# Second attention: maxima read from two PSUM banks and one in turn, and the values' products cut into two halves of 256 columns

## The reference

```python
query = qt_c + qt_r                   # each heads(...): (b, 16, 1024, 8)
key = kt_c + kt_r
attn = jnp.einsum('bhqd,bhkd->bhqk', query, key) / scale      # scale = 12
attn = jax.nn.softmax(attn, axis=-1)
out = jnp.einsum('bhqk,bhkd->bhqd', attn, value)
```

## Time and profile before

| what | us |
|---|---|
| median of three executions | 2005.73 |
| lowest, highest | 2004.09, 2005.89 |
| profiled execution, span from first to last instruction | 2004.5 |
| second attention, its maxima's first to last product | 1129.7 to 1808 |
| steps, from the first exponential to the last reduce of a maxima tile | 1172.8 to 1809 |

### The profile page before, as it was taken

One profiled execution on the slowest core, in us unless ns is written; L12 is line 12 of the kernel. 1 busy time (PEld: TensorE's weight loads), 2 busy tenths in 40 slices (PEclk: granted clock), 3 DMA queues, 4 the chain that ended last, 5 costly groups with the idle time before them and its releaser, 6 DMA issues. The chain is left out here.

```text
span 2004.5 us, 34034 instructions
## 1 busy us (share of the span) xinstructions
PE 1788.9 (89%) x12761; PEld 670.6 (33%) x12761; DVE 1459.2 (73%) x3121; ACT 1092.4 (54%) x1386; POOL 644.9 (32%) x776
## 2 busy tenths in 40 slices
PE   6878799999999999999599888888888888889897
PEld 3535333333333333333333332111211211112465
DVE  5866666666666667663444689999999999994743
ACT  4312244454455445545324158878887878887432
POOL 0033445445555555432224113203302500001153
PEclk8987999999999999999799899999999999999798
DMA  4000000000000000000121101211221212220114
GB/s 137 1 1 1 1 21 25 23 24 23 23 24 23 34 24 24 33 24 23 24 111 54 62 26 69 74 44 44 81 81 45 86 65 63 82 81 7 63 35 145
DMA packets 56673, 91.80 MB, mean 46 GB/s; under 512 B 21989, under 2 KB 30565, under 8 KB 56381
## 3 DMA queue, kind: packets, MB, share of 16 engines
q1 hardware_dynamic: 54940, 85.94, 12.4%
q0 software_dynamic: 1280, 2.62, 0.5%
q10 hardware_dynamic: 288, 1.05, 0.2%
HBM read 46.23 MB, written 38.51 MB: 42 GB/s over the span
## 5 line engine op out<-in xcount | busy, mean ns | idle before, releaser
L1853 DVE TENSOR_REDUCE h_m_half<-h_ps_max 128x1 f32<-128x512 f32 x1024 | 635.8, 682 | 32.4 <-PE h_ps_max L1460 29.7
L1709 ACT ACTIVATE h_P<-h_ps_st 128x1024 f32<-128x1024 f32 x512 | 497.8, 1023 | 86.6 <-PE h_ps_st L1476 84.0
L929 PE MATMUL l_ps_st<-l_Q,l_K 64*128 64x512 f32 (+3 forms) x1536 | 310.3, 498 | 4.2 <-DMA l_Q<-l_m_row 2.0
L1089 ACT ACTIVATE l_P<-l_ps_st 128x1024 f32<-128x1024 f32 (+3 forms) x256 | 207.7, 834 | 192.7 <-PE l_ps_st L929 192.0
L1180 DVE CUSTOM_DVE_ANT_0 l_masked<-l_ps_t,l_mask 128x384 bf16<-128x384 f32 (+3 forms) x512 | 229.3, 485 | 63.7 <-PE l_ps_t L883 63.6
L1486 PE MATMUL h_ps_o<-h_P,h_V 128*9 128x512 f32 x2048 | 267.7, 595 | 0.7 <-ACT h_P L1709 0.5
L1460 PE MATMUL h_ps_max<-h_K,h_Q 48*128 48x512 bf16 x1024 | 201.0, 389 | 66.7 <-DVE h_m_half L1853 64.7
L1183 DVE TENSOR_REDUCE l_m_half<-l_ps_t 128x1 f32<-128x512 f32 x256 | 164.5, 685 | 69.7 <-PE l_ps_t L883 68.3
L1476 PE MATMUL h_ps_st<-h_Q,h_K 51*128 51x512 bf16 x1024 | 167.4, 379 | 14.9 <-ACT h_P L1709 11.0
L1460 PEld LDWEIGHTS h_ps_max<-h_K,h_Q 48*128 48x128 bf16 x1024 | 49.2, 93 | 387.1 <-DVE h_m_half L1853 372.5
L1757 POOL CAST h_m_parts<-h_m_neg 128x16 bf16<-128x16 f32 x32 | 6.3, 198 | 517.3 <-DVE h_m_neg L1817 517.3
(11 more groups left out here) (469 smaller groups left out, 2416.2 us busy)
## 6 DMA issues: line engine op xcount, KB each, us to landing
sums<-l_o SPq DMA_DIRECT2D x15, 512.0 KB, 2.7
sums<-h_o SPq DMA_DIRECT2D x15, 512.0 KB, 2.6
h_K<-k_parts SPq DMA_DIRECT2D x32, 192.0 KB
h_Q<-q_parts SPq DMA_DIRECT2D x32, 192.0 KB
y_rows<-zero SPq DMA_DIRECT2D x8, 512.0 KB, 4.9
c_W<-c_W SPq DMA_DIRECT2D x32, 128.0 KB, 2.1
c_W<-in_W SPq DMA_DIRECT2D x16, 256.0 KB, 4.0
c_back<-y_rows SPq DMA_DIRECT2D x16, 256.0 KB, 5.6
```

The costliest lines, as they stand in the source:

```text
L929: last = pe.matmul(ps_st[x % 2][:, a, 0:w], K[n // NG % 2][rows, kt * 128:(kt + 1) * 128], Q[n % NQ][rows, c, p, q0 - c * CH:q0 - c * CH + ...
L1089: act.activation(P[e % PR][:, :, 0:w], ps_st[slot["s", n, i, p] % 2][:, :, 0:w], ACT.Exp, scale=0.125).then_inc(consumed, 1)
L1709: act.activation(P[e % PR][:, :, :], ps_st[x % 2][:, :, :], ACT.Exp, scale=1.0 / 12.0).then_inc(consumed, 1)
L1853: dve.tensor_reduce(m_half[:, half, 2 * p + a, qt:qt + 1], ps_max[:, t % NB, :], AX.X, ALU.max, negate=True)\
```

## The change

Tiles are grouped in units: a unit of two tiles (banks 0 and 1), then a unit of one (bank 2), in turn; 683 units for 1024 tiles. DVE reads a unit with one `tensor_reduce`, 1024 or 512 wide. PE may write unit k when unit k - 2 is reduced, and signals once a unit. The results go to `m_tiles`, laid out by tile; `settle` combines them with two instructions of half the size where one was.

`values(n, i, side)` does the four products of a step for 256 of the 512 columns; the two sides are called apart. `next_maxima` has four places in a step: 0 between the scores, 1 after them, 2 between the sides, 3 after the second side. BEAT says which are used: 0, 2, 3 in two steps of three, and 1, 2 in the third; eight units, twelve tiles, in three steps. Every step has place 2. AHEAD = 53 bounds how far maxima run ahead: a place is left empty when the next tile's number isn't below 53 + 4 times the step's number. A step with a projection or an output has place 3 in any case, and there and after its product the bound doesn't hold. SKIP is gone.

The lead has the same 48 tiles in 32 units: 21 units (12 with half a `normalise`, 9 with two idle products), then the 12 idle products and the first turn, then 11 units with two idle products each (8 pairs before).

```diff
-    LEAD, TURNS, INVERT_AT = 8, (6, 14), 8
+    TILES, UNITS = 2 * NPAIR, 2 * (2 * NPAIR * NGR // 3) + 1
+    LEAD, TURNS, INVERT_AT = 32, (6, 14), 8
+    BEAT, AHEAD = ((0, 2, 3), (0, 2, 3), (1, 2)), 53
-    NORM_AT = {2 * k: x for k, x in enumerate(NORM)}
+    NORM_AT = {k + k // 3: (NORM[k // 2], k % 2) for k in range(2 * len(NORM))}
+    NORM_AFTER = {k + 2: x for k, (x, half) in NORM_AT.items() if half}
+    def tiles_of(k):
+        t = 3 * (k // 2) + 2 * (k % 2)
+        return range(t, t + 1) if k % 2 or k == UNITS - 1 else range(t, t + 2)
...
+            def maxima(k):
+                if k >= 2:
+                    pe.wait_ge(reduced, k - 1)
+                for t in tiles_of(k):
...
+                    last = pe.matmul(ps_max[:, t % NB, :], Q[n % NBUF][rows, p, qt * 128:(qt + 1) * 128],
+                                     K[n % NBUF][rows, p, lo:lo + CH], start=True, stop=True)
+                last.then_inc(max_ready, 1)
...
+            def values(n, i, side):
...
                 for j in range(HG):
-                    last = pe.matmul(ps_o[32 * j:32 * j + M, :], V[b % 2][:, kt, g * HG + j, :],
-                                     P[(2 * (n * NI + i) + j // 2) % PR][:, j % 2, :], start=(kt == 0), stop=(kt == KT - 1))
-                last.then_inc(pv_done, 1)
+                    last = pe.matmul(ps_o[32 * j:32 * j + M, cols], V[b % 2][:, kt, g * HG + j, :],
+                                     P[(2 * (n * NI + i) + j // 2) % PR][:, j % 2, cols], start=(kt == 0 and side == 0), stop=(kt == KT - 1 and side == 1))
+                if side:
+                    last.then_inc(pv_done, 1)
...
                     scores(n, i, 0)
-                    if follows:
-                        next_maxima()
+                    if 0 in beat:
+                        next_maxima(most)
                     scores(n, i, 1)
-                    if not follows and (n, i) not in SKIP:
-                        next_maxima()
+                    if 1 in beat:
+                        next_maxima(most)
                     if n + i:
-                        values(n if i else n - 1, (i - 1) % NI)
-                    next_maxima()
+                        values(n if i else n - 1, (i - 1) % NI, 0)
+                    if 2 in beat:
+                        next_maxima(most)
+                    if n + i:
+                        values(n if i else n - 1, (i - 1) % NI, 1)
+                    if 3 in beat or key:
+                        next_maxima(most if key is None else 2 * NPAIR * NGR)
...
+                tiles = m_tiles[:, at:at + TILES // 2].rearrange("x (k p s a) -> x p a k s", k=KT // 2, p=2, s=2)
+                for p in range(2):
+                    last = dve.tensor_tensor(m_neg[c][:, 2 * p:2 * p + 2, :], tiles[:, p, :, :, 0], tiles[:, p, :, :, 1], ALU.min)
...
+            for k in range(UNITS):
+                t, count = tiles_of(k)[0], len(tiles_of(k))
+                at = t % (3 * TILES)
+                dve.wait_ge(max_ready, k + 1)
+                dve.tensor_reduce(m_tiles[:, at:at + count], ps_max[:, t % NB:t % NB + count, :], AX.X, ALU.max, negate=True).then_inc(reduced, 1)
```

More of the change, by code:

```diff
@@ L1292, in head_attention @@
             AT[(b - 1) * NG + k // 4, (1, 3, 9, 11)[k % 4]] = (x, b, c)
-            SKIP.add(((b - 1) * NG + k // 4, (5, 7, 13, 15)[k % 4]))
     for b in range(B - 1):
-        SKIP |= {((b + 1) * NG + g, i) for g in (2, 3) for i in (5,)}
         AT[(b + 1) * NG + 2, 2] = ("out", b, 0)
@@ L1448, in output @@
                 pe.matmul(to[:, 0, :], Wo[:, 0, :], packed[b % 2][:, c * CH:(c + 1) * CH], start=True, stop=True).then_inc(st_ready, 1)
[L1450 to L1461 removed]
+            def maxima(k):
+                if k >= 2:
+                    pe.wait_ge(reduced, k - 1)
+                for t in tiles_of(k):
+                    n, u, a = t // TILES, t // 2 % NPAIR, t % 2
+                    if u == 0:
+                        pe.wait_ge(loads[n % NBUF], 16 * NLOAD * (n // NBUF + 1))
+                    qt, p, lo, rows = u // 4, (u // 2) % 2, (u % 2) * CH, slice(64 * a, 64 * a + D6)
+                    last = pe.matmul(ps_max[:, t % NB, :], Q[n % NBUF][rows, p, qt * 128:(qt + 1) * 128],
+                                     K[n % NBUF][rows, p, lo:lo + CH], start=True, stop=True)
+                last.then_inc(max_ready, 1)
             def turn(h):
@@ L1554, in _ @@
             pe.matmul(ps_o[:, 0:1], Wo[:, 0, :], bv[:, 0:1], start=True, stop=True).then_inc(bias_made, 1)
-            for u in range(HALF):
-                maxima(0, u)
-                if u == 0:
+            for k in range(unit_of(TILES // 2 - 1) + 1):
+                maxima(k)
+                if k == 0:
                     pe.wait_ge(cleared, 1)
-                if u in NORM_AT:
-                    normalise(*NORM_AT[u], 0)
-                elif u - 1 in NORM_AT:
-                    normalise(*NORM_AT[u - 1], 1)
+                if k in NORM_AT:
+                    normalise(*NORM_AT[k][0], NORM_AT[k][1])
                 else:
@@ L1566, in _, with next_maxima @@
             turn(0)
-            for u in range(HALF, HALF + LEAD):
-                maxima(0, u)
+            for k in range(unit_of(TILES // 2 - 1) + 1, LEAD):
+                maxima(k)
                 idle_products(2)
-            pairs = iter(range(HALF + LEAD, NGR * NPAIR))
-            def next_maxima():
-                v = next(pairs, None)
-                if v is not None:
-                    maxima(v // NPAIR, v % NPAIR)
+            todo = list(range(UNITS - 1, LEAD - 1, -1))
+            def next_maxima(before=2 * NPAIR * NGR):
+                if todo and tiles_of(todo[-1])[0] < before:
+                    maxima(todo.pop())
             for n in range(NGR):
@@ L1604, in _ @@
                         ln_center_early(*LN_AT[i])
-            values(NGR - 1, NI - 1)
+            for side in range(2):
+                values(NGR - 1, NI - 1, side)
             pe.wait_ge(ln_moved, 4)
```

62 lines of the change are left out of this document (24 added, 38 removed).

## The result

The kernel with the change takes 2016.5 us (median of four executions, 2014.7 to 2019.4) and the kernel before, on the same chip, 2005.8 (2004.1 to 2006.0). The ratio is 1.0056, with an interval of 1.0044 to 1.0068: slower by 0.6%, where no change was forecast. The profiled spans are 2013.1 and 2004.5 us.

What follows compares the result with a forecast made beforehand. A loop over DVE and PE was taken to bound the step, 2.47 us before and after. Steps 0, projections -1.5 + 3.5, outputs -1.2, lead -1.4 gave -0.6 on a span of 2004.5: median 2005, range 1982 to 2019.

Steps and rivals of the forecast that it cites:

- the four stretches: Ordinary steps, from one unit of two to the next: 1.99, 1.70, 1.73 and 1.98 us, three steps 7.40.
- cheaper changes of tiling: Rival, around the halves: changes cost half of 0.10, so 0.14 us a step less, 1981; chance 0.30 with milder forms.
- a dearer fixed part of the reads: Rival, DVE's PSUM reads: fixed cost as on the skill's page, 0.08 us a step gained, 1992; chance 0.02.
- reads over two banks without gain: Slower rival, DVE's wide reduces: 1.20 between starts, +0.05 us a step, 2017; chance 0.14 shared with late weights.
- late weights: Slower rival, each half's second pass on PE: 0.05 late, +0.07 us a step, 2020; chance 0.14 shared with reads over two banks without gain.
- Groups with projections: Steps with projections or outputs: "ka" and "ct" -1.5 us, "x" and "y" +3.5, outputs -1.2.
- the bound of 53 leaves one unit, 1.93: Step behind a "ka" or "ct" product: one unit left, 1.93 us; with the product's step 5.91 for 6.54.
- +0.45 ahead of an "x" or "y": PE's way to an "x" or "y" product: two tiling changes and a unit more ahead of it, +0.45 us.
- The lead: Code ahead of the steps: +0.6 us behind the first turn, that turn 2.0 earlier, sum -1.4.
- with its gaps filled (about 3.8 of 4 by the same chain) I take it that the clock stays: Lead, at 1144 to 1148: PE busier than 2.29 of 4 us, keeping full clock, first turn 2.0 us earlier.
- the lead keeps its half clock: Slower rival, lead: five more units at 1.7 us and no earlier turn, +6 for -2, 2012; chance 0.14.
- `settle` and turns: Ordinary steps: the second `settle` instruction, the inversion and the turns fall half into idle time; steps' change 0.

Runs made afterwards that it cites:

- scores twice: Kernel before, with the second pair of score products made twice in the six groups with projections; 2013.3 us, ratio 1.0041.
- the third: Changed kernel with a third instruction of the same size in each `settle`, its result unused; 2016.9 us, one execution.
- e1: Kernel before, with values in two halves, maxima still in pairs, one between the scores and one between the halves, in every group; 2013.7 us, ratio 1.0038.

## Why the prediction was wrong

**What held.** Every price of the ordinary loop: the reduces, the halves, the changes of tiling, the four stretches, 2.47 a step. The sum over DVE (busy 592, forecast 590) and PE's becoming the fuller engine too. Of the rivals, cheaper changes of tiling (0.30), a dearer fixed part of the reads (0.02) and, under the last 0.14, reads over two banks without gain (1.73 and not 1.80 from double to double) and late weights (a half leaves 0.55 and not 0.61) were shut out by the same rows.

**What failed: the step "Groups with projections".** It was 0.8 for all groups with products (-1.5 + 3.5 - 1.2), and measured 8.5 (6.8 + 0 + 1.7). Taken apart by ACT's exponentials:

| steps | measured, us | forecast |
|---|---|---|
| "x", "y": the product's and the one behind | +1.2 | +1.4 |
| "x", "y": i = 6, 7, 14, 15 | +2.9 | +2.4 |
| "x", "y": i = 0, 5, 8, 13 | +2.6 | 0 |
| "ka", "ct": i = 0 to 5 and 8 to 13 | -2.9 | -4.0 |
| "ka", "ct": i = 6, 7, 14, 15 | +2.9 | +2.4 |
| outputs: i = 2 and 3 | -1.3 | -3.8 |
| outputs: all others | +2.9 | +2.6 |

The forecast's column is from its own terms: for "x" and "y" they add up to 3.8 where it wrote 3.5, and the last row is what its -1.2 leaves.

Three terms were wrong.

First, in the groups of "x" and "y" the steps i = 0, 5, 8 and 13 were left at no change. They were short before (2.30 at i = 0 and 8, 2.42 at i = 5 and 13, for 2.47), and after they have units by the beat: in group 5 they are 2.57, 2.75, 2.59 and 2.43 (i = 0, 5, 8, 13).

Second, the forecast has one unit in the step behind a product ("the bound of 53 leaves one unit, 1.93"), and gives the pair 5.91 for 6.54 everywhere. The time was right, 1.89; the count was not. By the kernel's own lists one unit is left behind 14 of the 30 products, and two behind the other 16. Which it is depends on where the product falls in the beat of three steps, and a group's 16 steps shift this by one. PE's timeline of group 4 has both, the step i = 2 and the step i = 4:

```profile
1346.92 0.48 PE L1468 MATMUL h_ps_max<-h_K,h_Q 48*128 48x512 bf16 x2
1347.75 1.05 PE L1496 MATMUL h_ps_o<-h_P,h_V 128*9 128x256 f32 x16
1348.73 0.39 PE L1485 MATMUL h_ps_st<-h_Q,h_K 51*128 51x512 bf16 x2
...
1353.45 0.38 PE L1468 MATMUL h_ps_max<-h_K,h_Q 48*128 48x512 bf16 x1
1353.76 0.62 PE L1496 MATMUL h_ps_o<-h_P,h_V 128*9 128x256 f32 x8
1354.31 0.39 PE L1468 MATMUL h_ps_max<-h_K,h_Q 48*128 48x512 bf16 x2
1354.63 0.62 PE L1496 MATMUL h_ps_o<-h_P,h_V 128*9 128x256 f32 x8
1355.19 0.39 PE L1485 MATMUL h_ps_st<-h_Q,h_K 51*128 51x512 bf16 x2
```

With one unit, ahead of the values, the halves run on as sixteen records; the step is 1.89. With two, one stands between the halves, and it is 2.55 (2.33 where the other unit stands between the scores). The six outputs took 1.89, 2.33 and 2.55 twice each, before 2.55 in five of them, so as a pair they gained 1.3 and not six times 0.63. The first half of group 4, which the forecast worked out, came right: from i = 0 to i = 6 it is 1358.04 - 1340.67 = 17.37, and 17.3 was forecast. Taking it for every half was the error.

Third, the steps behind that chain. ACT's timeline of group 4 after, i = 6, 7 and 8, for the earlier trace rows:

```profile
1358.04 1.94 ACT L1724 ACTIVATE h_P<-h_ps_st 128x1024 f32<-128x1024 f32 x2
1360.44 1.94 ACT L1724 ACTIVATE h_P<-h_ps_st 128x1024 f32<-128x1024 f32 x2 [0.46 <-PE h_ps_st L1485]
1362.80 1.02 ACT L1724 ACTIVATE h_P<-h_ps_st 128x1024 f32<-128x1024 f32 x1 [0.43 <-PE h_ps_st L1485]
```

The two are 1362.80 - 1358.04 = 4.76 (4.98 in the group's second half), forecast 4.6. Before they were 4.29 and 4.38, not the 4.2 of the forecast, which took half a group less 17.97; the halves are not equal. They have the full beat and are ordinary steps: the tiles had been left out earlier, directly behind the products.

What stands behind this was tested. Halves at the products and behind them cost 5.0 us (whole values at the products, 668.7 for 673.7); the forecast's chain carried a part of this (+0.45 ahead of an "x" or "y"). Load on PE costs a third of itself in these groups (scores twice): all of it in the step behind a product and at i = 6, nothing at i = 0 and 5. That the steps SKIP made light can't be had back in another place with this beat was tried in one way only (maxima left out later). The other 4.4 us of the steps are, in the kernel with whole values at the products, 1.6 in groups with projections, 1.8 in those with an output and 1.0 in the plain ones; they go with the full beat in steps that were light, and with the second `settle` instruction, but how they divide was not measured.

**The lead (-1.4, measured +1.8).** The step "with its gaps filled (about 3.8 of 4 by the same chain) I take it that the clock stays" failed. Windows of the lead after, for the earlier trace rows:

```profile
1142.00:1146.00 4.00, 3.56 (x34) 2.21 (x31) 4.00 (x6) 0.00 (x0) 0.00 (x0) 1.00 0.00 0
1146.00:1158.00 12.00, 12.00 (x53) 8.20 (x52) 9.51 (x12) 2.29 (x2) 0.75 (x4) 0.57 0.01 2
```

PE is busy 3.56 of 4 us (2.29 before), and the granted clock still falls from full (2.4 GHz) to half in the 12 us behind it. The first turn comes 33.7 us after the first maxima product, for 33.2, not 2.0 earlier, and from it to the first exponential it is 11.2 for 9.9, +1.3 where +0.6 was forecast. That is the rival "the lead keeps its half clock", but at +1.8 and not +6. The half clock lasted less long: by these rows 0.43 x 12 / 0.5 = 10.3 us, for some 13 before. How much that gave back, and how much the smaller units did, was not measured. Behind the turn PE's timeline has a unit every 0.96 us, for the 0.92 of the sum:

```profile
1159.91 0.39 PE L1468 MATMUL h_ps_max<-h_K,h_Q 48*128 48x512 bf16 x1
...
1160.87 0.39 PE L1468 MATMUL h_ps_max<-h_K,h_Q 48*128 48x512 bf16 x2
...
1161.84 0.39 PE L1468 MATMUL h_ps_max<-h_K,h_Q 48*128 48x512 bf16 x1
```

**`settle` and turns (0).** +1.0 over the four plain groups. If the second instruction costs what the third did, it explains some 0.4 of this; the rest is open.

So the median, 2016.5, lies inside the range (1982 to 2019) by luck: it reaches so far up for rivals at 2017 and 2020, reads without gain and late weights, and neither took place. The forecast's own 2001 to 2009 missed it, since the steps that weren't ordinary were priced from one case of each and not by their place in the beat.

## What to carry to other kernels

Here the ordinary step of a loop closed over two engines stayed at 2.47 us, as priced, and the irregular steps made the result. So price them (with an extra product, behind it, and those made light to pay for it) one by one, and not the ordinary one alone; and where a pattern has another period than the loop (here three steps against 16), go through every place at which they meet, since one case doesn't stand for all. When one of two parts of a change can be had without the other, try it so: here halves in ordinary steps and whole values elsewhere gained 0.3%, while a wide reduce saved DVE 0.07 us over two small ones and gained the loop nothing. Idle products are worth counting again where the clock falls in spite of them.

## What was unexpected in the hardware

- The granted clock fell to half in the lead although PE was busy 3.56 of the 4 us before. Twelve idle products at the lower clock cost more than they gave: with 4 for 12 the lead is 2.8 us shorter (43.1 to 40.3) and the steps as long (657.6 for 657.9). Only some 2.2 of the 2.8 can be put down to them: both this kernel and e1, whose lead is the one of before, had the clock at 0.50 for 17 us (1144.3 to 1161.4, and 1145.2 to 1162.3), and the lead of e1 is 42.5.
- A single unit's product, on one half of the rows, starts with a score product on the other half: 1734.57 and 1734.58 in the trace after. By the signals in the trace that score product is the second of its pair; the first, which needs the single's half, starts at 1734.80. So here a product on a free half of the rows started ahead of an earlier one on the busy half.
- By their lengths a wide reduce (1219 ns) is 540 more than a small one (679), so 139 ns don't depend on the size. But the next read starts before the end: from start to start it is 1.13 to 1.14 for a wide one and 0.60 for a small one, so only some 0.07 us are saved by joining two. The Trainium skill (VectorE: DVE Perf Modes, the table of cycles) has 120 cycles for a PSUM read's fixed part, 0.125 us as an estimate: near the one from the lengths, and twice what a stream of reads gives back. The measurement decides.
- The Trainium skill says that a change of tiling drains the engine (TensorEngine Tiling (Array Packing), Key Properties), which speaks against putting bf16 products on half of the rows between value products on a quarter of the columns. The traces agree in the times, though they don't show a drain as such: from a maxima product it is 0.31 us to the values and 0.22 to a score; a half leaves 0.55 to a maxima product, and 0.44 to its other half where the two are adjacent; and whole values gained back 0.21 us a product.
